# Local attention in a four-layer kernel: probabilities scaled before the weighted sum, output made with channels on the partitions

## What is computed

```python
HEADS, DIM_HEAD, WINDOW, INNER = 8, 64, 64, 512
q, k, v = split(shift_token(x) @ wqkv)             # 8 heads of 64
q, k = rotary_xpos(l2norm(q) * qs, l2norm(k) * ksc)
# every block of 64 queries looks at its own 64 keys and at the 64 before them
sim = einsum('bhwid,bhwjd->bhwij', 8 * bq, bk)     # masked outside the window
attn = softmax(sim, axis=-1)
o = einsum('bhwij,bhwjd->bhwid', attn, bv)         # 1024 x 512
x = x + o @ wo
x = x + ffn(layer_norm(shift_token(x)))            # 128 -> 2*341 -> gated gelu -> 128
```

## Time and profile before

| | |
|---|---|
| median of 3 runs | 4187.87 us (4178.26 to 4192.16) |
| the profiled execution | 4199.19 us, its span 4197.2 us |
| PE busy | 3672.0 us, 87% of the span |
| DVE busy | 2642.6 us, 63% |
| ACT busy | 2150.7 us, 51% |
| POOL busy | 864.7 us, 21% |
| granted TensorE clock, mean | 0.94 |

### The profile page before, as it was taken

One profiled execution on the slowest core, in us unless ns is written; L12 is line 12 of the kernel. 1 busy time (PEld: TensorE's weight loads), 2 busy tenths in 40 slices (PEclk: granted clock), 3 DMA queues, 4 the chain that ended last, 5 costly groups with the idle time before them and its releaser, 6 DMA issues. The chain is left out here.

```text
span 4197.2 us, 81504 instructions
## 1 busy us (share of the span) xinstructions
PE 3672.0 (87%) x30800; PEld 2073.2 (49%) x30800; DVE 2642.6 (63%) x5977; ACT 2150.7 (51%) x4957; POOL 864.7 (21%) x1071
## 2 busy tenths in 40 slices
PE   5988878888989996799899999998988998888987
PEld 3655654444545453334333343345655665555555
DVE  5667646565565554776777777736655665664755
ACT  3555544545555454365565665653554554444454
POOL 1111001000010001213233142125213231431421
PEclk8999988989989898799999999999999999999999
DMA  3221311111111101101111011002120230320212
GB/s 110 61 49 40 72 26 50 36 29 24 36 26 44 25 17 61 51 22 48 29 41 36 24 38 34 23 31 73 37 62 23 62 82 8 80 63 26 60 38 54
DMA packets 149549, 183.63 MB, mean 44 GB/s; under 512 B 34568, under 2 KB 102216, under 8 KB 145832
## 3 DMA queue, kind: packets, MB, share of 16 engines
q1 hardware_dynamic: 143268, 171.01, 15.7%
q10 hardware_dynamic: 5892, 7.41, 0.7%
HBM read 91.69 MB, written 34.08 MB: 30 GB/s over the span
## 5 line engine op out<-in xcount | busy, mean ns | idle before, releaser
L1361 ACT ACTIVATE prob<-ps_st 128x512 f32<-128x512 f32 (+3 forms) x2432 | 1123.4, 510 | 1105.9 <-PE ps_st L1298 588.2
L1394 DVE TENSOR_REDUCE mhalf<-mx 128x1 f32<-128x512 f32 (+3 forms) x2064 | 1252.7, 650 | 574.9 <-PE mx L1335 320.6
L1332 PE MATMUL mx<-ks,qs 56*128 56x512 bf16 (+4 forms) x2304 | 630.5, 368 | 122.8 <-DVE g_tok L1969 52.5
L1269 PE MATMUL ps_st<-qs,ks 59*128 59x512 bf16 (+4 forms) x2432 | 622.9, 353 | 51.8 <-ACT prob L1361 37.0
L1255 PE MATMUL ps_o<-prob,vst 128*32 128x256 f32 (+3 forms) x7416 | 621.5, 415 | 1.3 <-ACT prob L1361 0.6
L1332 PEld LDWEIGHTS mx<-ks,qs 72*128 72x128 bf16 (+1 forms) x2304 | 193.4, 101 | 388.2 <-DVE mhalf L1394 73.1
L1269 PEld LDWEIGHTS ps_st<-qs,ks 75*128 75x128 bf16 (+1 forms) x2432 | 192.7, 98 | 373.0 <-ACT prob L1361 235.4
L1255 PEld LDWEIGHTS ps_o<-prob,vst 128*32 128x32 f32 x7416 | 154.6, 110 | 258.6 <-issue 127.0
L1444 POOL COPY vst<-v_tok 128x256 f32<-128x256 f32 x48 | 19.8, 416 | 1168.1 <-PE ps_o L1255 1152.3
L3317 ACT ACTIVATE o<-ps,nm,lrq 128x128 f32<-128x128 f32 x512 | 226.7, 459 | 33.4 <-DVE nm L3432 22.6
L1276 PE MATMUL ps_st<-qx,kx 64*128 64x512 bf16 x1024 | 208.9, 389 | 0.0
(11 more groups left out here) (488 smaller groups left out, 6555.0 us busy)
## 6 DMA issues: line engine op xcount, KB each, us to landing
qs<-q_scr SPq DMA_DIRECT2D x186, 96.0 KB
ks<-k_scr SPq DMA_DIRECT2D x90, 192.0 KB
lkt<-o SPq DMA_DIRECT2D x256, 64.0 KB, 2.0
lve<-lv SPq DMA_DIRECT2D x24, 512.0 KB, 4.7
lqt<-o SPq DMA_DIRECT2D x160, 64.0 KB, 2.1
tabs<-local_tables SPq DMA_DIRECT2D x4, 2048.0 KB, 8.4
k_scr<-part SPq DMA_DIRECT2D x30, 256.0 KB, 3.2
lqt<-o ACTq DMA_DIRECT2D x96, 64.0 KB, 2.2
```

The costliest lines, as they stand in the source:

```text
L1269: return nc.tensor.matmul(score_bank(GH * b + n)[:, 0:q1 - q0], ks[g % 2][row:row + R + 3, lane, kt * P:(kt + 1) * P], qs[g % 2][row:row + ...
L1332: last = nc.tensor.matmul(bank[:, j * w:(j + 1) * w], qs[g % 2][row:row + R, hf, lane, (t - 4 * hf) * P:(t - 4 * hf + 1) * P], ks[g % 2][r ...
L1361: nc.scalar.activation(prob[:, b % PROBS, h, 0:q1 - q0], ps_st[:, u % 3, 0:q1 - q0], ACT.Exp, scale=scale).then_inc(S["exped"], 1)
L1394: nc.vector.tensor_reduce(mhalf[:, hf, h0:h0 + heads, t - 4 * hf, part], bank[:, 0:heads * (k1 - k0)].rearrange("p (n w) -> p n w", n=head ...
```

## The change

The probabilities are scaled before the weighted sum and not its result after it. `normalise`, `turn_out` and the copy on ACT are gone. Instead DVE takes the reciprocals for each unit (`inverse`), GpSimd multiplies the unit's four probability matrices with them in place (`scale`), and `weigh` has its operands swapped: the values are the stationary side and the transposed probabilities move, so that `po` comes out with channels on the partitions. `channels` is now a copy on DVE from `po` to `och`. The rows of `wo` are ordered to fit on the host (`LOCAL_OUT`). The probabilities have four buffers (slots 0 and 3 of `o`), and the orders on PE and DVE are written anew: `maxima` runs two tiles ahead, and `project` follows its tile by one and not by two.

```diff
-            pr, ptr = (o[:, k, :, :].rearrange("p s (i c) -> p s i c", i=4) for k in range(2))
+            pr = [four(o[:, k, g, :]) for k in (0, 3) for g in range(2)]
+            ptr = [four(o[:, 1, g, :]) for g in range(2)]
...
                     def turn(u):
...
-                        pe.wait_ge(S["exped"], 4 * (u + 1))
-                        if g == 0 and t >= 2:
-                            pe.wait_ge(S["ch"], t - 1)
+                        pe.wait_ge(S["scaled"], u + 1)
+                        if u >= 2:
                             pe.wait_ge(S["copied"], u - 1)
+                        if u % 2 == 0 and u >= 4:
+                            pe.wait_ge(S["sum"], u // 2 - 1)
...
-                                last = nc.tensor.matmul(po[w * WINDOW:(w + 1) * WINDOW, t % 2, h * D:(h + 1) * D],
-                                                        ptr[:, u % 2, i, w * WINDOW:(w + 1) * WINDOW], v[:, t, h * D:(h + 1) * D],
-                                                        start=True, stop=True)
+                                    last = nc.tensor.matmul(po[D * e:D * e + D, t % 2, c0:c0 + WINDOW], v[:, t, h * D:(h + 1) * D],
+                                                            ptr[u % 2][:, i, w * WINDOW:(w + 1) * WINDOW], start=True, stop=True)
...
                     for t in range(NT):
                         turn(2 * t)
-                        turn(2 * t + 1)
                         if t + 2 < NT:
                             scores(t + 2)
+                        if t >= 1:
+                            weigh(2 * t - 1)
+                        turn(2 * t + 1)
+                        if t >= 1:
+                            project(t - 1)
                         weigh(2 * t)
-                        if t >= 1:
-                            turn_out(t - 1)
-                        weigh(2 * t + 1)
-                        if t >= 2:
-                            project(t - 2)
...
                         act.wait_ge(S["max"], u + 1)
                         if u == 0:
                             act.wait_ge(placed[0], 256)
-                        if u >= 2:
-                            act.wait_ge(S["tp"], u - 1)
-                        if g == 0 and t >= 2:
-                            act.wait_ge(S["inv"], t - 1)
+                        if u == 2:
+                            act.wait_ge(placed[3], 256)
+                        if u >= 4:
+                            act.wait_ge(S["tp"], u - 3)
+                            act.wait_ge(S["inv"], u - 3)
...
+                    def inverse(u):
+                        dve.wait_ge(S["exped"], 4 * (u + 1))
+                        if u >= 4:
+                            dve.wait_ge(S["scaled"], u - 3)
+                        nc.vector.reciprocal(inv[:, u % 4, :], den[:, u % 4, :]).then_inc(S["inv"], 1)
...
                     for t in range(NT):
-                        if t >= 1:
-                            normalise(t - 1)
-                        if t >= 3:
-                            residual(t - 3)
-                        if t + 1 < NT:
-                            maxima(2 * t + 2)
                         copies(2 * t)
                         if t + 1 < NT:
-                            maxima(2 * t + 3)
+                            inverse(2 * t + 2)
+                        if t + 2 < NT:
+                            maxima(2 * t + 4)
+                        if t >= 1:
+                            channels(t - 1)
                         copies(2 * t + 1)
+                        if t + 1 < NT:
+                            inverse(2 * t + 3)
+                        if t + 2 < NT:
+                            maxima(2 * t + 5)
+                        if t >= 1:
+                            residual(t - 1)
...
+                    def scale(u):
+                        pool.wait_ge(S["inv"], u + 1)
+                        nc.gpsimd.tensor_tensor(pr[u % 4], pr[u % 4], inv[:, u % 4, :].unsqueeze(2).broadcast_to([P, 4, P]),
+                                                ALU.mult).then_inc(S["scaled"], 1)
```

More of the change, by code:

```diff
@@ L80 @@
 LOCAL = np.concatenate([LOCAL_QK, 512 + LOCAL_QK, 1024 + np.arange(512)])
+LOCAL_OUT = np.array([64 * (2 * (2 * (j % 2) + e) + j // 2) + k for j in range(4) for e in range(2) for k in range(64)])
 def halves(v):
@@ L2967, in local_block @@
                                  "k_spread", "k_unit", "placed0", "placed1", "placed2", "placed3", "small", "both", "edge",
-                                 "s", "raw", "max", "exped", "tp", "copied", "o", "inv", "norm", "turned", "ch", "mm", "sum", "low", "first", "sent",
+                                 "s", "raw", "max", "exped", "inv", "scaled", "tp", "copied", "o", "ch", "mm", "sum", "low", "first", "sent",
                                  "shifted", "high", "stat", "var", "spread", "std", "rstd", "unit", "unit_t", "in_ch", "hid", "gelu", "gated",
@@ L3173, in turn @@
                     def turn(u):
-                        t, g = units[u]
                         if u == 0:
@@ L3213, in weigh, with project @@
                         last.then_inc(S["o"], 1)
-                    def turn_out(t):
-                        pe.wait_ge(S["norm"], t + 1)
-                        if t + 1 < NT:
+                    def project(t):
+                        pe.wait_ge(S["ch"], t + 1)
+                        if t < NT - 1:
                             pe.wait_ge(S["copied"], 2 * t + 3)
                         else:
-                            pe.wait_ge(S["ch"], t)
+                            pe.wait_ge(S["copied"], 2 * NT)
+                        if 1 <= t < NT - 1:
+                            pe.wait_ge(S["sum"], t)
+                        to = pt[:, 0 if t < NT - 1 else 1, 0:C]
@@ L3221, in turn_out @@
                         for j in range(4):
-                            last = nc.tensor.transpose(pt[:, 0, j * P:(j + 1) * P], o_tok[:, t % 2, j * P:(j + 1) * P], net.ident)
-                        last.then_inc(S["turned"], 1)
-                    def project(t):
-                        pe.wait_ge(S["ch"], t + 1)
-                        if t + 2 < NT:
-                            pe.wait_ge(S["copied"], 2 * t + 6)
-                        else:
-                            pe.wait_ge(S["sum"], t)
-                        for j in range(4):
-                            last = nc.tensor.matmul(pt[:, 1, 0:C], och[:, t % 2, j * P:(j + 1) * P], W(f"l3_wo{d}", 4, j),
-                                                    start=(j == 0), stop=(j == 3))
+                            last = nc.tensor.matmul(to, och[:, t % 2, j * P:(j + 1) * P], W(f"l3_wo{d}", 4, j), start=(j == 0), stop=(j == 3))
@@ L3462, in _ @@
                     inverse_q(1)
+                    inverse(0)
+                    maxima(2)
+                    inverse(1)
+                    maxima(3)
                     for t in range(NT):
-                        if t >= 1:
-                            normalise(t - 1)
-                        if t >= 3:
-                            residual(t - 3)
-                        if t + 1 < NT:
-                            maxima(2 * t + 2)
                         copies(2 * t)
                         if t + 1 < NT:
-                            maxima(2 * t + 3)
-                        copies(2 * t + 1)
-                    normalise(NT - 1)
-                    residual(NT - 3)
+                            inverse(2 * t + 2)
[3 more added lines that the diff above has]
+                            channels(t - 1)
+                        copies(2 * t + 1)
+                        if t + 1 < NT:
[4 more added lines that the diff above has]
+                            residual(t - 1)
+                    channels(NT - 1)
                     dve.wait_ge(S["sent"], 32)
@@ L3478, in _ @@
                     spreads(0)
-                    residual(NT - 2)
                     to_units(0)
@@ L3514, in _, with lows @@
                     nc.gpsimd.memset(late[0:1, 0, HC:C], 0.0).then_inc(S["first"], 1)
-                    for t in range(NT):
+                    def scale(u):
+                        pool.wait_ge(S["inv"], u + 1)
+                        nc.gpsimd.tensor_tensor(pr[u % 4], pr[u % 4], inv[:, u % 4, :].unsqueeze(2).broadcast_to([P, 4, P]),
+                                                ALU.mult).then_inc(S["scaled"], 1)
+                    def lows(t):
                         pool.wait_ge(S["sum"], t + 1)
                         nc.gpsimd.tensor_copy(late[:, t, 0:HC], net.xn_tok[:, t, 0:HC]).then_inc(S["low"], 1)
+                    for u in range(2 * NT):
+                        scale(u)
+                        if u % 2 == 1 and u >= 5:
+                            lows((u - 5) // 2)
+                    for t in range(NT - 2, NT):
+                        lows(t)
                     pool.wait_ge(S["low"], NT)
```

76 lines of the change are left out of this document (27 added, 49 removed).

## The result

The changed kernel takes 4221.11 us (median of 4 runs, 4217.63 to 4235.7) against 4190.01 for the kernel before (median of 4, 4178.26 to 4195.23): a ratio of 1.0071, 95% interval 1.0049 to 1.0093. The prediction was 4198, range 4182 to 4214, so the result lies outside, on the slow side. The profiled execution takes 4235.7 us, its span is 4233.3.

The account below looks back on a forecast made before the run. It took a cycle of PE's turn, scores, weigh, turn_out and ACT's copy and exponentials as the bound, to be replaced by a DVE-PE loop. 8 x (0.2 + 1.0) + 0.8 = +10.4 us gave 4198, range 4182 to 4214.

Parts of the forecast that it names:

- 5.41 us for a tile instead of 5.78: Middle tiles of attention: a DVE and PE loop from first maxima to scores closes each tile in 5.41 us.
- maxima 0.79: DVE's term in the tile loop: each unit's maxima take 0.79 us, counted twice per tile.
- costs nothing in the middle: GpSimd's scale in middle tiles: 1.27 us, hidden because inverse to turn leaves some 4 us.
- Rival 3: GpSimd becomes the bound through sharing with DVE, scale 2.6 us or more: about +40 us, 4228; chance 0.06.
- +14.4 us forecast: Stage up to the statistics: 0.7 us later and 1.0 of clock per block, 0.8 more in the first.
- The 0.3 us a block: Stage's end: added to the counted 46.7 us because the count of before gave 45.8 against the trace's 46.3.
- Unit 2 waits for piece 7: Stage start: unit 2's exponentials wait until piece 7 leaves slot 3 of `o`, 2.5 us late, 3.3 in first block.
- The clock falls behind PE's gap: PE idle 3.3 us ahead of turn(2), then half clock: 0 to 1.6 us a block, 1.0 taken, every block.
- The square root's table load: Behind the statistics: ACT has loaded the table by then, which gives back 0.5 us a block.
- Rival 1: The clock costs nothing, its stretch ending early or falling where DVE and ACT set the pace: +2.4 us, 4190; chance 0.17.
- Rival 2: PE's clock stays low for 6.8 us, costing 2.6 a block: +23 us, 4211; chance 0.21.
- Rival 4: Piece 7 is away sooner, its issues 0.6 us apart, PE's gap gone: -18 us, 4170; chance 0.07.

Follow-up runs that it names:

- the kernel with it busy: Kernel before plus three unused GpSimd subtractions of 128x512 behind each tile's normalisation: 4211.8 us, ratio 1.0036 to the kernel before.
- the three experiments: Changed kernel with inverse behind second maxima, 4210.55 us; with scale in two instructions, 4207.61; with inverse behind second maxima and probability buffers 2, 3 in `in_ch`, 4181.35.
- Both together in the kernel before: Kernel before with one wait added, unit 2's exponentials waiting for piece 7: 4226.87 us, ratio 1.0075 to the kernel before.
- With the hold taken away: Changed kernel with the second unit's inverse moved behind its maxima on DVE: 4210.55 us, ratio 1.0022 to the kernel before.
- the filled gap: Changed kernel with twelve unused matmuls on PE ahead of turn(2): 4212.19 us, ratio 1.0034 to the kernel before.
- the order was worth more: Changed kernel, buffers 2 and 3 in `in_ch`, second weigh ahead of turns, channels first, residual ahead of second maxima: 4147.49 us, ratio 0.9883 to before.
- the halves: Changed kernel with each GpSimd scale made as two instructions of two heads: 4207.61 us, ratio 1.0019 to the kernel before.

## Why the prediction was wrong

**The step that failed** is "5.41 us for a tile instead of 5.78": tiles take 5.82. The loop was named rightly, and DVE is the one waited for; its term "maxima 0.79" holds for the first unit (0.81) and not for the second, where it is 1.14 (3330.29 to 3331.43). Behind it stands the sentence that the scale "costs nothing in the middle", a term put at nothing: the runs price it at 12.7 us. I weighed GpSimd's length and its share of time, not what it does to DVE while it runs.

Rival 3 named the sharing but took its size from the wrong side, as a GpSimd slowed to 2.6 us. In this stage GpSimd isn't slowed (1038 to 1042 ns in the kernel with it busy): DVE is. There I cited the Trainium skill (GPSIMD Engine Reference, section 8), contention with DVE instructions that have two SBUF inputs, and judged by their size that there is next to none. The trace agrees with the rule and not with my use of it: the price is what is left of the GpSimd instruction, which drew the 0.16 us out to 1.00 here, however small DVE's instruction is. The inverse stands 0.8 us ahead of the multiplication, so the second multiplication of a tile falls inside the scale that the inverse released.

The trace of the kernel before had the sign already. Eight of its 128 multiplications, the first of each block, last 0.35 us beside a GpSimd subtraction or addition; they are the maximum in 161/163/355 above, and the rows stand in the last section. The row that gave the upper bound for the scale, L2768 at 0.72 us, is a mean of two sorts, 12 of 0.61 and 20 of 0.79 us, and the longer ones lie beside such DVE instructions too.

In numbers, to the statistics: +14.4 us forecast (8 x 0.7, 8 x 1.0, 0.8), +31.0 measured. The hold makes 12.7 of the 16.6 between them (11.6 to 14.1 by the three experiments). The tile without the hold, 5.46 against 5.41, makes about 2 more (8 x 5 x 0.05). The clock was 0.8 cheaper. Some 3 us are left that no run settles. The 0.3 us a block that the prediction adds to its count of the stage's end stands on a count of the kernel before that no row shows, which fell 0.5 short.

**What held.** Unit 2 waits for piece 7: 7.61 behind the first exponential on average, against 7.4 to 8.1 forecast, and 2.65 later than before against 2.5; blocks spread from 6.2 to 8.7. The clock falls behind PE's gap (3.85 us in block 1, 3.10 in block 3, against 3.3), in seven blocks where the prediction had eight, and costs 0.9 against 1.0. Both together in the kernel before cost 29.1 against 28.8. The square root's table load is away: it ends at 2986.37 in block 1, the root starts at 2993.63, 0.03 behind its input's end (2993.43 + 0.17). From the statistics to the first product behind the feed-forward's activation, six blocks get back 0.5 to 0.7 us each against the 0.5 forecast. Blocks 4 and 7 lose 0.9 and 0.2 instead, with a granted clock of 0.50 in that stretch, so that only 2.6 us are left in all. The swapped weigh keeps its time: one of its matmuls takes 0.23 us on average in both kernels. With the hold taken away the kernel is at +9 us by its ratio of 1.0022, where the forecast was +10.4; but the interval reaches from 0 to 18 us, and the stage is 16.5 us longer than before where 14.4 were forecast, so the closeness is partly luck.

**The rivals.** Rival 1 falls with the filled gap: the clock costs 7.2 us. Rival 2's fall of 6.8 us came behind PE's gap in block 1 alone. Rival 4 fails on the 7.93 us in which SP issues, about as long as before (8.07). Rival 3's mechanism decided, with DVE and GpSimd exchanged.

## What to carry to other kernels

Work given to an idle GpSimd has a price on VectorE even where nobody waits for it: look in the timeline for DVE instructions that work in SBUF alone beside it, with two inputs or as a `tensor_scalar`, however small, and charge them the rest of the GpSimd instruction. The hold shows neither as idle time nor as a wait, only in the longest and median duration of such an instruction. Then place them out of its reach, as here by making the release of GpSimd (the inverse) the last thing and not the first. And where a change frees one loop, write the order of all engines for the next one: here the order was worth more (32.5 us with the hold already away) than the hold and the clock together (12.7 and 7.2).

## What the runs showed of the hardware

A small DVE instruction with two SBUF inputs that starts beside a GpSimd `tensor_tensor` lasts until that one instruction ends: 0.16 us became 0.33, 0.47, 0.53 and 1.00, each time to within some 0.02 us of that end. DVE instructions with an input in PSUM weren't held beside the same work (reduction 0.68, residual 0.29), nor was the reciprocal of 128x4 (0.17 beside it and alone).

It isn't only instructions with two inputs. In the kernel before, in the timeline of DVE and then of POOL:

```profile
2929.38 0.35 DVE L3432 TENSOR_TENSOR nm<-nm,lrq 128x4 f32<-128x4 f32 x1
...
2987.59 1.09 DVE L3405 TENSOR_SCALAR std<-mv 128x4 f32<-128x4 f32 x1
```
```profile
2927.21 2.50 POOL L3510 TENSOR_TENSOR o<-o,v_tok 128x512 f32<-128x512 f32 x2 [0.33 <-DVE v_tok L3385]
...
2986.16 2.50 POOL L3523 TENSOR_TENSOR xn_tok<-xn_tok,stream 128x512 f32<-128x512 f32 x2
```

The `tensor_scalar` has one tensor input, in SBUF as its output is, and takes 0.17 us in the same block with GpSimd idle. Beside the addition it takes 1.09 and ends at 2988.68, 0.02 behind GpSimd's 2988.66.

A larger DVE instruction runs on behind the end of GpSimd's, and then GpSimd's next one is drawn out as well. In the third layer of the kernel before, in the timelines of DVE and POOL and in the line of L2768 (durations in ns as above):

```profile
2853.74 0.94 DVE L2875 TENSOR_TENSOR sdec<-state,m_etot 64x256 f32<-64x256 f32 x1
```
```profile
2853.61 0.79 POOL L2782 TENSOR_TENSOR m_y<-m_y,m_z 128x256 f32<-128x256 f32 x1
2854.37 0.79 POOL L2768 TENSOR_TENSOR xdt<-m_x,m_dt 128x256 f32<-128x256 f32 x1
```
```profile
L2768 POOL TENSOR_TENSOR xdt<-m_x,m_dt x32: 612/788/795, 2844.3 to 3925.8; 128x256 f32<-128x256 f32 x32
```

L2875 takes 0.41 us with GpSimd idle. Here it takes 0.94 and ends 0.28 behind L2782, and L2768, which starts in that time, takes 0.79 in place of 0.61. So either engine can wait for the other; in the attention stage of the changed kernel no scale starts while such a DVE instruction runs, so there only DVE waited.

GpSimd's 128x512 multiplication with one operand broadcast along the inner elements takes 1.04 us, and so does a subtraction whose two operands are the same; the addition and subtraction of two different tensors take 1.27. With 128x256 elements it is 0.61 with the broadcast (the halves) and 0.72 with two different tensors (L2780), so the gap grows with the size. What makes it was not tried.
